# Splitting row maxima on the way out of PSUM, and queries ahead of indirect writes, in a fused decoder layer

## What is computed

```
q, k, v = x @ wq.T, x @ wk.T, x @ wv.T          # self: q and k are rotated (rope); cross: biases, k and v from the context
scores  = q @ k.T / 4                           # 256 x 256 for each head; cross: masked keys get -1e9
attn    = softmax(scores)                       # needs the row maximum of every query and head
out     = attn @ v
x       = layernorm(x + out)                    # cross: out @ Wo.T + bo first
...
gates   = softmax(x @ router_w + router_b)      # top 2 of 8 experts, position in the expert by a running count
buf     = rows of x placed at (expert, position), at most 1280 for an expert
y       = gates * (gelu(buf @ w1 + b1) @ w2 + b2), gathered;  x = layernorm(x + y)
```

## Time and profile before

| | |
|---|---|
| three runs | 2308.83, 2306.36, 2310.83 us |
| the profiled execution's own time | 2308.35 us |
| its span, first to last instruction | 2306.1 us |
| busy: PE, DVE, ACT, POOL | 2091.8, 1383.5, 993.1, 838.7 us |
| granted TensorE clock, mean | 0.959 of full speed |
| one pair of half-steps in the steady part | 51.2 us |
| attention stage | to about 1710 us; the experts follow |

### The profile page before, as it was taken

One profiled execution on the slowest core, in us unless ns is written; L12 is line 12 of the kernel. 1 busy time (PEld: TensorE's weight loads), 2 busy tenths in 40 slices (PEclk: granted clock), 3 DMA queues, 4 the chain that ended last, 5 costly groups with the idle time before them and its releaser, 6 DMA issues. The chain is left out here.

```text
span 2306.1 us, 55186 instructions
## 1 busy us (share of the span) xinstructions
PE 2091.8 (91%) x21891; PEld 1546.1 (67%) x21891; DVE 1383.5 (60%) x2900; ACT 993.1 (43%) x1515; POOL 838.7 (36%) x1102
## 2 busy tenths in 40 slices
PE   7899999899989999999899999997879999999996
PEld 4666666666666666666666666665548787787775
DVE  5677777777777777777777777775421111111136
ACT  2455455555544555555445555553412212212233
POOL 3334334444443344444433444442332121221244
PEclk8999999999999999999999999999879999999998
DMA  3331111111000000010000000100021333323454
GB/s 90 110 123 31 36 49 49 33 53 40 26 32 32 28 26 26 29 32 23 26 28 25 23 23 29 32 24 19 14 66 28 80 85 76 71 30 78 85 182 167
DMA packets 99532, 118.81 MB, mean 52 GB/s; under 512 B 12144, under 2 KB 92221, under 8 KB 97232
## 3 DMA queue, kind: packets, MB, share of 16 engines
q1 hardware_dynamic: 69856, 83.75, 11.4%
q0 software_dynamic: 17184, 19.66, 4.8%
q10 hardware_dynamic: 12240, 11.88, 1.5%
HBM read 66.11 MB, written 56.12 MB: 53 GB/s over the span
## 5 line engine op out<-in xcount | busy, mean ns | idle before, releaser
L869 ACT ACTIVATE prob<-ps_e 128x1024 f32<-128x1024 f32 x508 | 520.1, 1024 | 527.2 <-PE ps_e L674 431.6
L990 DVE TENSOR_REDUCE smax<-ps_s 128x4 f32<-128x1024 f32 x508 | 618.5, 1218 | 207.4 <-PE ps_s L661 202.4
L661 PE MATMUL ps_s<-stack_kh,stack_q 32*128 32x256 f32 x2032 | 304.9, 306 | 0.8 <-ACT stack_q L858 0.8
L1826 ACT ACTIVATE hid<-m_ps_h,b_sb 128x320 f32<-128x320 f32 x256 | 134.7, 527 | 392.2 <-PE m_ps_h L1780 392.2
L674 PE MATMUL ps_e<-stack_q,stack_kh 32*128 32x256 f32 x2032 | 295.5, 281 | 0.0
L674 PE MATMUL ps_e<-stack_q,stack_kl 32*128 32x256 f32 x2032 | 292.4, 277 | 0.0
L1780 PE MATMUL m_ps_h<-m_cols,w_sb 128*128 128x320 f32 x1024 | 290.7, 433 | 0.6 <-DVE m_cols L1849 0.6
L1797 PE MATMUL m_ps_o<-w_sb,hid 128*128 128x256 f32 x1280 | 279.1, 379 | 1.3 <-DVE m_res L1878 1.3
L661 PE MATMUL ps_s<-stack_kl,stack_q 32*128 32x256 f32 x2032 | 276.2, 278 | 0.0
L618 PE MATMUL ps_w<-ident,padded 128*128 128x128 f32 x1024 | 178.3, 301 | 106.5 <-POOL padded L1277 103.1
L1797 PEld LDWEIGHTS m_ps_o<-w_sb,hid 128*128 128x128 f32 x1280 | 243.1, 190 | 36.4 <-DVE m_res L1878 1.7
(11 more groups left out here) (170 smaller groups left out, 3740.3 us busy)
## 6 DMA issues: line engine op xcount, KB each, us to landing
w_sb<-in_w SPq DMA_DIRECT2D x16, 1024.0 KB, 7.0
slot_rows_dram<-w_sb ACTq DMA_DIRECT2D x40, 258.0 KB, 2.7
m_rows<-slot_rows_dram SPq DMA_DIRECT2D x15, 645.0 KB, 5.7
xT<-in_xT SPq DMA_DIRECT2D x32, 256.0 KB, 2.8
ctxT<-in_ctxT SPq DMA_DIRECT2D x32, 256.0 KB, 2.8
x_res<-in_x SPq DMA_DIRECT2D x32, 256.0 KB, 2.9
sums_dram<-x SPq DMA_DIRECT2D x32, 256.0 KB, 2.1
c_rows<-sums_dram SPq DMA_DIRECT2D x8, 1024.0 KB, 15.4
```

Source lines behind the costliest of these rows:

```text
L661: return nc.tensor.matmul(out, stack_q[at_side][rows, g, t * P:(t + 1) * P], (stack_kh, stack_kl)[part][at_side][rows, g, :], start=(X == ...
L869: nc.scalar.activation(prob[:, h:h + 2, :].rearrange("p h s -> p (h s)"), shifted[:, :, :, :].rearrange("p h t s -> p (h t s)"), ACT.Exp, ...
L990: nc.vector.tensor_reduce(max_columns(X, p), scores[:, :, :, :], AX.X, ALU.max)\
L1826: nc.scalar.activation(hid[:, m, half * HALF:(half + 1) * HALF], ps_h[:, (2 * m + half) % 4, 0:HALF], ACT.Gelu, bias=b1_sb[:, pe_, m:m + 1 ...
```

## The change

Three edits. First, on POOL `query_parts` of a CROSS item stands ahead of `scatter`. Second, DVE no longer splits the maxima in SBUF. PE transposes `smax` whole (16 rows); ACT copies these out of PSUM in the fast format (`max_high`, semaphore `high_ev`), and DVE then subtracts that copy from the same PSUM rows (`max_remainders`, into `max_low`, semaphore `rest_ev`). SP sends the two parts from the two tiles. Third, the order and the waits that go with it: `max_remainders` stands at k = 5 for half 1 of e and at k = 13 for half 0 of s; `maxima` at k = 0 and 8 waits until `smax` of the last item of its kind is transposed; and the reader of a "max_rows" bank is now `rest_ev`.

```diff
--- before.py
+++ after.py
@@ -187,8 +187,8 @@
         aux_cross = sb("aux_cross", [P, MASK_TILES, S], F32R)
         val = [sb(f"val{side}", [P, T2, H, 32]) for side in range(2)]
         smax = [sb(f"smax{t}", [P, T2 * H]) for t in (SELF, CROSS)]
-        smax_parts = [sb(f"smax_parts{t}", [P, 2, PARTS, H]) for t in (SELF, CROSS)]
-        nrows = [[sb(f"nrows{t}{half}", [PARTS * H, P], F32R) for half in range(2)] for t in (SELF, CROSS)]
+        max_high = [[sb(f"max_high{t}{half}", [H, P], F32R) for half in range(2)] for t in (SELF, CROSS)]
+        max_low = [[sb(f"max_low{t}{half}", [H, P], F32R) for half in range(2)] for t in (SELF, CROSS)]
         prob = sb("prob", [P, H, 2 * S])
         outT = [sb(f"outT{t}", [P, 4, S]) for t in (SELF, CROSS)]
         rden = sb("rden", [P, T2, H])
@@ -254,7 +254,6 @@
         masks_mm = steps("masks_mm", 1)
         masks_ev = steps("masks_ev", 1)
         aux_made = ctx.enter_context(nc.semaphore("aux_made"))
-        max_split = both("max_split", 2 * PARTS)
         low_ev = both("low_ev", 2)
         x2_sent = steps("x2_sent", 16)
         filled = steps("filled", 5)
@@ -283,7 +282,8 @@
         s_mm = both("s_mm", DUOS)
         s_max = both("s_max", H)
         neg_mm = both("neg_mm", 2)
-        neg_ev = both("neg_ev", 2)
+        high_ev = both("high_ev", 2)
+        rest_ev = both("rest_ev", 2)
         e_mm = both("e_mm", DUOS)
         e_exp = both("e_exp", H)
         pv_mm = both("pv_mm", 2)
@@ -429,7 +429,7 @@
                 "pv": (pv_ev[T], b, k + 1), "out_rows": (ln[T], b, 2 + 2 * k), "values": (v_ev[T], b, 1),
                 "columns": (col_ev[T], b, 1), "project_out": (ln[CROSS], b, 5), "x2_columns": (x2T_ev, b, 1),
                 "route": (r_ev, b, 1), "count": (count_ev, b, 2),
-                "project": (qk_ev[T], b, (k + 1) * qk_ev[T].per // T2), "max_rows": (neg_ev[T], b, k + 1),
+                "project": (qk_ev[T], b, (k + 1) * qk_ev[T].per // T2), "max_rows": (rest_ev[T], b, k + 1),
                 "stack_k": (low_ev[T], b, k + 1), "stack_q": (tr_ev[T], b, 2 * k + 2), "masks": (masks_ev, 0, 1),
             }[name]
 
@@ -486,12 +486,12 @@
 
             def place_maxima(T, b, half):
 
-                sp.wait_ge(neg_ev[T].sem, neg_ev[T].count(b, half + 1))
                 if max_in[T].due(b - 1):
                     sp.wait_ge(max_in[T].sem, max_in[T].count(b - 1))
-                for part in range(PARTS):
+                for part, (made, rows) in enumerate(((high_ev[T], max_high[T][half]), (rest_ev[T], max_low[T][half]))):
+                    sp.wait_ge(made.sem, made.count(b, half + 1))
                     sp.dma_start(aux_q[side((T, b))][MAX_ROW + part:P:STRIP, 2 * half:2 * half + 2, :].bitcast(F32),
-                                 nrows[T][half][part * H:(part + 1) * H, :].bitcast(F32)).then_inc(max_in[T].sem, 16)
+                                 rows[:, :].bitcast(F32)).then_inc(max_in[T].sem, 16)
 
             def store_masks():
                 sp.wait_ge(masks_ev.sem, masks_ev.count(0))
@@ -764,10 +764,9 @@
                   .then_inc(count_mm.sem, 1)
 
             def max_rows(X, b, half):
-                pe.wait_ge(max_split[X].sem, max_split[X].count(b, PARTS * (half + 1)))
+                pe.wait_ge(s_max[X].sem, s_max[X].count(b, H // 2 * (half + 1)))
                 take_bank("max_rows", X, b, half)
-                nc.tensor.transpose(work("max_rows", X, half)[0:PARTS * H, 0:P],
-                                    smax_parts[X][:, half, :, :].rearrange("p c h -> p (c h)"),
+                nc.tensor.transpose(work("max_rows", X, half)[0:H, 0:P], smax[X][:, H * half:H * (half + 1)],
                                     ident[:, :]).then_inc(neg_mm[X].sem, 1)
 
             def masks_by_row():
@@ -882,7 +881,7 @@
                 act.wait_ge(neg_mm[X].sem, neg_mm[X].count(b, half + 1))
                 if max_in[X].due(b - 1):
                     act.wait_ge(max_in[X].sem, max_in[X].count(b - 1))
-                nc.scalar.copy(nrows[X][half][:, :], work("max_rows", X, half)[0:PARTS * H, 0:P]).then_inc(neg_ev[X].sem, 1)
+                nc.scalar.copy(max_high[X][half][:, :], work("max_rows", X, half)[0:H, 0:P]).then_inc(high_ev[X].sem, 1)
 
             def masks_by_row():
                 act.wait_ge(masks_mm.sem, masks_mm.count(0))
@@ -987,19 +986,19 @@
 
             def maxima(X, b, p, scores):
                 dve.wait_ge(s_mm[X].sem, s_mm[X].count(b, p // 2 + 1))
+                if p % (H // 2) == 0:
+                    if neg_mm[X].due(b - 1, p // (H // 2) + 1):
+                        dve.wait_ge(neg_mm[X].sem, neg_mm[X].count(b - 1, p // (H // 2) + 1))
                 nc.vector.tensor_reduce(max_columns(X, p), scores[:, :, :, :], AX.X, ALU.max)\
                   .then_inc(s_max[X].sem, 2)
 
-            def split_maxima(X, b, half):
-
-                dve.wait_ge(s_max[X].sem, s_max[X].count(b, H // 2 * (half + 1)))
-                if neg_mm[X].due(b - 1, half + 1):
-                    dve.wait_ge(neg_mm[X].sem, neg_mm[X].count(b - 1, half + 1))
-                whole, high = smax[X][:, H * half:H * (half + 1)], smax_parts[X][:, half, HIGH, :]
-                nc.vector.tensor_copy(high.bitcast(F32R), whole).then_inc(max_split[X].sem, 1)
-                dve.wait_ge(max_split[X].sem, max_split[X].count(b, PARTS * half + 1))
-                nc.vector.tensor_tensor(smax_parts[X][:, half, LOW, :], whole, high, ALU.subtract)\
-                  .then_inc(max_split[X].sem, 1)
+            def max_remainders(X, b, half):
+
+                dve.wait_ge(high_ev[X].sem, high_ev[X].count(b, half + 1))
+                if max_in[X].due(b - 1):
+                    dve.wait_ge(max_in[X].sem, max_in[X].count(b - 1))
+                nc.vector.tensor_tensor(max_low[X][half][:, :], work("max_rows", X, half)[0:H, 0:P],
+                                        max_high[X][half][:, :].bitcast(F32), ALU.subtract).then_inc(rest_ev[X].sem, 1)
 
             def key_remainders(Y, b, half):
 
@@ -1190,10 +1189,12 @@
                 for k in range(H):
                     if s is not None and k % 2 == 0:
                         maxima(*s, k, score_tile(s, e, k // 2))
-                    if s is not None and k in (H // 2 - 1, H - 1):
-                        split_maxima(*s, k // (H // 2))
                     if s is not None and k == 5:
                         key_remainders(*s, 1)
+                    if e is not None and k == 2 * MAX1 + 3:
+                        max_remainders(*e, 1)
+                    if s is not None and k == 2 * MAX0 + 3:
+                        max_remainders(*s, 0)
                     if n is not None and k == 2 * slot_of(STACK_K, LATE_STACK_K, n) + 3:
                         key_remainders(*n, 0)
                     if h == 0 and k == 3:
@@ -1395,11 +1396,11 @@
                     pool.wait_ge(masks.sem, masks.count(0))
                 if is_of(CROSS, n):
                     masked_keys(n[1])
+                if is_of(CROSS, n):
+                    query_parts(*n)
                 settled = item(h - 5)
                 if is_of(CROSS, settled) and settled[1] < NB - 3:
                     scatter(settled[1])
-                if is_of(CROSS, n):
-                    query_parts(*n)
                 if is_of(SELF, n):
                     turned_parts(n[1])
                 if is_of(CROSS, r):
```

## The result

The changed kernel takes 2395.39 us (median of 4 runs, 2388.84 to 2402.41) against 2309.02 us (4 runs), a ratio of 1.0375 with a 95% interval of 1.0344 to 1.0407. It is 86 us slower. The forecast was 28 us slower (2337 us), with the upper end of the range at 2405.

A forecast was written before the change was run, and what follows sets the result against it. PE bounds the kernel, 91% busy: 2306.1 - 103 - 42 + 137 - 22 = 2276 us, plus 59 us for clock falls gives a 2335 us span, so 2337 us, 1.2% slower; range 2270 to 2405 us.

The forecast's parts named there:

- the reader of a bank decides: PE's stack_q after duo 2 must wait for DVE's subtraction to free its PSUM bank: 63 half-steps, +137 us.
- The subtraction: DVE's new instruction on the maxima, 16 x 128 out of PSUM: 0.30 us, bounds 0.2 and 0.42 us.
- The short waits: PE's short waits from DVE's lateness, 28.4 and 15.2 us: half of them go, -22 us.
- The DMA of the low part: Maxima's low part lands near 808.1 us, before duo 4 needs it; hidden by the new bank wait, costing nothing.
- Edit 1 at -145 us: Queries ahead of POOL's indirect DMAs: stack_q's wait goes whole, -103 us, plus -42 us of clock.
- two falls for three gaps: New gaps before stack_q in duo 2: clock falls 42 times at 1.4 us each, +59 us.
- the stretch at 62.5 us: Trace before, early: after PE worked 1.56 of 2.50 us, the clock fell to 0.50 for 10.2 us.
- the upper bound: Clock term for the new gaps at its worst: all 63 fall with twice the cost, +176 us.
- edit 1's clock: Without the wait for the queries, 30 clock falls at 1.4 us each vanish: -42 us.
- The clock holds: Rival: the shorter new gaps bring only 0 to 20 falls, 2278 to 2306 us; chance 0.23.
- The clock falls and stays down: Rival: 42 to 63 falls behind the new gaps at 2.8 us each, 2396 to 2454 us; chance 0.16.
- all 63 gaps: Skill's rule applied to the new bank waits: every gap brings a fall, 88 us, 2364 us in place of 2335.

The follow-up runs named there:

- edit 1 alone: The kernel before with only the queries split ahead of the indirect writes on POOL: 2165.16 us, ratio 0.9366 to before.
- The filled kernel: The changed kernel with eight unused bf16 matmuls issued just ahead of stack_q in duo 2, the bank wait kept: 2295.94 us, ratio 0.9938 to before.
- the run with the other bank: The changed kernel with three uses of the PSUM banks rotated in duos 2 and 3, nothing else: 2179.52 us, ratio 0.943 to before.
- the run of edits 2 and 3 alone: The changed kernel with POOL's indirect writes put back ahead of the query split, leaving the maxima part: 2528.03 us, ratio 1.0945 to before.

## Why the prediction was wrong

**What was right.** The bound and the place: PE, and its wait in the earlier trace rows. That the reader of a bank decides: 137 us forecast, 137.0 in 63 waits measured, 2.30 and 2.04 us in A and B where 2.31 and 2.05 were worked out. The subtraction: 0.27 us where 0.30 was taken. The short waits: -17.8 us where -22 was taken. The DMA of the low part was hidden, as said. The direction. Edit 1 at -145 us came out at -144.8 alone, but that it is so close is partly luck. Between the profiled executions PE's idle time fell by 98.2 us (4.2 us of the wait stay, at the start) and its busy time by 38.2 us, where 103 and 42 were taken; that is 136.4 us, and the other 8 are that the profiled execution of edit 1 alone took 2171.85 us, above its median, and that of before a little less than its own.

**What failed** is one term, "I take two falls for three gaps: 42 falls, at 1.4 us each as above, +59 us". The filled kernel puts it at 99.5 us and PE's busy time at 97.1. The number of falls was near (45), which is worth 4 us. The price was not: 2.2 us on average. It was read from one kind of fall, which ended after 3.4 us with 3.1 us of work in it. For the falls of that length it was nearly right, 1.4 us where the runs show 1.7, because behind the gap in A no part of the fall lies in idle time. But 18 of the 45 last 6.8 us, nearly all behind the gap in B, and cost 3.1 us each; they make some 30 of the 38 to 40 us that the term is short. Both could be seen as possible in the stretch at 62.5 us; I kept that for the upper bound and priced the sum by the gentler row.

The profiled execution closes the sum. Its span is 2386.7 us, 52 more than the 2335 of the forecast: 38 for the falls, 4 for edit 1's wait that stayed, 4 for edit 1's clock, 4 for the short waits, and 6 for waits for sources (5.8 us, where no row of before had shown any), less 4 us by which other short waits of L672 fell. The median lies another 6.5 us above that execution, whose clock of 0.932 was also the highest of the four (0.926 to 0.932). Why B's falls last longer than A's stays open.

**The rivals.** "The clock holds" falls: 45 falls for 63 gaps. "The clock falls and stays down" was half right: 18 of 45 falls lasted 6.8 us. It named 2396 us as its lower end, and the median is 2395. That is partly luck, since it priced every fall at 2.8 us, and 27 of them cost 1.7. The rule of the Trainium skill, that waits for PSUM banks between groups of matmuls make the clock fall again and again ("TensorE: Matmul & The Clock Gate", "A second HAM failure mode: psum-queue depth-cycling"), agrees with the changed kernel, and the run with the other bank shows its converse: 8 falls without the bank wait. The forecast's reading of it, all 63 gaps, does not: in the run of edits 2 and 3 alone, 25 of 26 bank waits in A passed without a fall. And the trace of before wasn't quite without a bank wait to compare, as the forecast had it: L580 waits twice for DVE's `att` to leave its bank, 3.3 us in all at 1570 to 1603 us, and the next falls come over 19 us later.

## What to carry to other kernels

When an evacuation moves to another engine, follow the PSUM bank first: find the next user in PE's order, and where on the new engine the reader stands relative to it. Two steps in an engine's written order, or three rotated uses of each half-step in a table of banks, were worth over 210 us here, while the two ways to split the maxima came out the same.

Price an idle gap of TensorE as the wait plus its clock, and take the clock's price from how much work runs at half speed behind the gap. A fall twice as long cost about twice as much here, 3.1 against 1.7 us, so a price read from short falls needs the longer one beside it. Where two kernels have the same matmuls, the difference of PE's busy times is the clock's share and the rest is waiting; filler matmuls in the gap told the two apart here with the same result (99.5 and 97.1 us).

## What the runs showed that I had not expected

The clock's share is far from linear in the gap: with 63 gaps of 2.2 us it was 99.5 us, with 63 of 1.6 us about 19 us, and with gaps of 0.4 us or less behind filler matmuls the pair ran at 1.00. Nor does the gap's length alone decide: the same gap in A (2.3 us) was followed by a fall 27 times in 29 in the changed kernel and once in 26 when the queries were late too. What decides it then, no run here shows.

A fall can come after the gap. At 793.9 to 796.4 us PE was nearly idle at 1.00, and the clock went to 0.50 only with PE back at work, for 3.3 us.
